# Edge stage: tile numbers and turns worked out in registers from two numbers a chunk, and the softmax links placed at later steps

## The reference, cut to what matters

```python
feat_src, feat_dst, feat_v = (feat @ W + b).reshape(N, HEADS, OUT_FEATS)   # three weights
e = el[src] + er[dst];  e = where(e >= 0, e, 0.2 * e)
e_max = segment_max(e, dst)
exp_e = exp(e - e_max[dst])
a = exp_e / maximum(segment_sum(exp_e, dst)[dst], 1e-16)
rst = segment_sum(feat_v[src] * a[:, :, None], dst)
x = x + rst + mix(xn);  x = x + ffn(layernorm(x))
```

## Time and profile before

| what | us |
|---|---|
| median of three runs | 3512.27 (3508.56 to 3518.39) |
| the profiled execution, its own time | 3480.26 |
| its span | 3478.4 |
| projection begins on TensorE | 99.85 |
| edge stage, first `turned_hot` to the last (L1124, 52 times) | 815.8 to 2376.1 |
| granted TensorE clock, mean over the span | 0.809 |

### The profile page before, as it was taken

One profiled execution on the slowest core, in us unless ns is written; L12 is line 12 of the kernel. 1 busy time (PEld: TensorE's weight loads), 2 busy tenths in 40 slices (PEclk: granted clock), 3 DMA queues, 4 the chain that ended last, 5 costly groups with the idle time before them and its releaser, 6 DMA issues. The chain is left out here.

```text
span 3478.4 us, 50828 instructions
## 1 busy us (share of the span) xinstructions
PE 2417.5 (69%) x11245; PEld 1803.3 (52%) x11246; DVE 1829.6 (53%) x3903; ACT 909.8 (26%) x1917; POOL 1338.1 (38%) x1406
## 2 busy tenths in 40 slices
PE   3899998666777877777877777777233329999500
PEld 3677776223555555555555555555233328888400
DVE  5544443786666655566556655565353334444433
ACT  0111111011333333333333333333443313333100
POOL 0000000302565555565556555652144342222244
PEclk8899998898888878888788878889555559999755
DMA  3122222644555555655656556653655634444576
GB/s 115 49 68 68 68 68 77 228 167 134 165 162 159 157 164 163 169 160 154 169 164 171 166 154 173 170 163 89 221 134 136 131 76 134 145 145 145 168 257 232
DMA packets 238264, 507.89 MB, mean 146 GB/s; under 512 B 50320, under 2 KB 76432, under 8 KB 238208
## 3 DMA queue, kind: packets, MB, share of 16 engines
q0 software_dynamic: 85936, 274.85, 28.6%
q1 hardware_dynamic: 134752, 196.94, 18.5%
q10 hardware_dynamic: 17520, 35.44, 3.0%
HBM read 394.73 MB, written 112.37 MB: 146 GB/s over the span
## 5 line engine op out<-in xcount | busy, mean ns | idle before, releaser
L618 POOL DMA_INDIRECT arena<-v_table,idx x832 | 917.2, 1102 | 847.1 <-PE ps L1566 670.1
L1566 PE MATMUL ps<-arena 128*128 128x260 f32 x3328 | 975.4, 441 | 315.9 <-issue 289.6
L1566 PEld LDWEIGHTS ps<-arena 128*128 128x128 f32 x3328 | 678.5, 216 | 533.2 <-issue 427.7
L757 ACT ACTIVATE arena<-ps x832 | 501.9, 603 | 1096.2 <-PE ps L1566 668.4
L1182 DVE TENSOR_TENSOR arena<-arena 128x512 f32<-128x512 f32 x832 | 547.1, 683 | 0.0
L1384 PE MATMUL ps<-arena 128*128 (+4 forms) x1994 | 423.8, 336 | 94.3 <-DMA arena<-q_table 73.8
L1389 PE MATMUL ps<-ident,arena 128*128 128x128 f32 x1128 | 213.8, 308 | 328.1 <-DVE arena L1257 257.2
L1384 PEld LDWEIGHTS ps<-arena 128*128 128x128 f32 (+1 forms) x1994 | 275.7, 195 | 224.8 <-issue 115.3
L1389 PEld LDWEIGHTS ps<-ident,arena 128*128 128x128 f32 x1128 | 151.0, 159 | 349.3 <-DVE arena L1257 262.2
L658 POOL DMA_INDIRECT arena<-xn_table,e_idx x105 | 99.3, 945 | 281.5 <-PE ps L1389 265.0
L595 POOL TENSOR_SCALAR ag<-ag 128x1 f32<-128x1 f32 x49 | 10.7, 219 | 502.3 <-DVE ag L999 502.2
(11 more groups left out here) (282 smaller groups left out, 3470.0 us busy)
## 6 DMA issues: line engine op xcount, KB each, us to landing
y_table<-arena SPq DMA_DIRECT2D x105, 256.0 KB, 2.5
arena<-local_table ACTq DMA_DIRECT2D x52, 512.0 KB, 4.2
arena<-in_x SPq DMA_DIRECT2D x98, 256.0 KB, 2.7
arena<-v_table,idx POOLq DMA_INDIRECT x832
v_table<-arena SPq DMA_DIRECT2D x49, 260.0 KB, 2.9
agg<-arena SPq DMA_DIRECT2D x49, 260.0 KB
arena<-agg SPq DMA_DIRECT2D x49, 260.0 KB, 4.6
x_mix<-arena SPq DMA_DIRECT2D x49, 256.0 KB, 2.7
```

Of the source, the lines that this page charges most:

```text
L618: pool.indirect_dma_start(vg[:, j % 2 * U + i, :], None, v_table, bass.IndirectOffsetOnAxis(ap=idx[:, j, i:i + 1], axis=0))\
L757: act.activation(halves(fin[:, bass.ds(dst_, DH)], HALF), halves(ps[:, bass.ds(src_, 2 * D)], D)[:, :, 0:HALF], ACT.Copy).then_inc(s("act_ ...
L1566: last = pe.matmul(ps[:, bass.ds(acc + h * D, HALF)], hot[:, i // V % 2, i % V, :], vg[:, b * U + i, h * HALF:(h + 1) * HALF], start=False ...
```

## The change: two numbers a chunk, and other places for the links

- The per-step tables go. Two tables with one entry a chunk take their place: `first_tab`, the node tile of the chunk's first step, and `turn_tab`, 16 bits that say which steps are turns. A loop turn of two chunks reads both (`chunk_places`): four entries of each on TensorE, two of each on VectorE and ScalarE.
- From them each engine works out the turn (`turn_of`: shift and mask), the next tile (`next_tile`: add), the accumulator (`room_of`: mask and product), and ScalarE the places and counts of `snapshot`. `tile_tab`, the step that ends each tile, stays and moves by one entry; a turn on TensorE reads it.
- A snapshot no longer waits for the matmul of its own step; it waits for the count of closed accumulators that its tile asks for.
- VectorE's links move: `scored` from behind step 2 to 5, `run_max` 4 to 7, `linked` 6 to 9, `joined_max` 9 to 11, `shifted` 12 to 13. TensorE's: `turned_e` 1 to 5, `gathered_ends` 3 to 7, `spread_ends` 5 to 9, `turned_max` 8 to 12, `factors` 10 to 11. ScalarE's: `factor` from behind snapshot 4 to 10, `weights` 10 to 12.
- VectorE makes the first `hot` tile of a chunk ahead of its wait for the exponentials, not behind it.
- The store count `fin_st` shares another semaphore.

```diff
-def chunks(eng, body, bases=None):
+def chunks(eng, body, places, ahead):
 
     for c in range(2):
-        body(c, c, 0, *(bases(c, 2) if bases else ()))
+        body(c, c, 0, places(c, ahead + 1))
     with eng.Fori(1, NCH // 2 - 1) as i:
-        own = bases(i * 2, 3) if bases else ()
+        own = places(i * 2, ahead + 2)
         for j in range(2):
-            body(i * 2 + j, j, i, *own[j:j + 2])
+            body(i * 2 + j, j, i, own[j:j + ahead + 1])
     for c in range(NCH - 2, NCH):
-        body(c, c % 2, c // 2, *(bases(c, 2) if bases else ()))
+        body(c, c % 2, c // 2, places(c, ahead + 1))
+
+
+def turn_of(eng, bits, i):
+
+    return eng.snap((bits >> i) & 1, min_val=0, max_val=1)
+
+
+def room_of(eng, d):
+
+    return eng.snap((d & 1) * (2 * D), min_val=0, max_val=2 * D)
+
+
+def next_tile(eng, d, turn):
+
+    return eng.snap((d + turn).with_bounds(min_val=0, max_val=NT - 1))
...
+        def chunk_places(engine, c, n):
+
+            return list(zip(looked_up(engine, first_tab, c, n, NT - 1), looked_up(engine, turn_tab, c, n, 2 ** U - 1)))
...
-            def snapshots(t, n):
-                places = looked_up(ENGINE.Activation, act_tab, t * 2, 2 * n, DUMMY * D)
-                counts = looked_up(ENGINE.Activation, act_tab, t * 2 + 2 * ST, 2 * n, 32768)
-                for i in range(n):
-                    (src_, dst_), (closed, stored) = places[2 * i:2 * i + 2], counts[2 * i:2 * i + 2]
-                    act.wait_ge(s("step_mm"), t + (i + 1))
-                    if later(t, 1) or i:
-                        act.wait_ge(s("act_step"), t + i)
-                    act.wait_ge(s("tile_sum"), closed)
-                    act.wait_ge(s("fin_st"), stored)
-                    act.activation(halves(fin[:, bass.ds(dst_, DH)], HALF), halves(ps[:, bass.ds(src_, 2 * D)], D)[:, :, 0:HALF],
-                                   ACT.Copy).then_inc(s("act_step"), 1)
-
-            def chunk(c, b, r):
+            def snapshot(t, d, turn):
+                src_ = act.snap(DUMMY * D - (DUMMY * D - (d & 1) * (2 * D)) * turn, min_val=0, max_val=DUMMY * D)
+                dst_ = act.snap(4 * DH - (4 * DH - (d & 3) * DH) * turn, min_val=0, max_val=4 * DH)
+                closed = act.snap(d + turn + 1, min_val=1, max_val=NT + 1)
+                stored = act.snap(d * 16 + past("fin_st", -16 * 3)[1], min_val=16, max_val=32768)
+                if later(t, 1):
+                    act.wait_ge(s("act_step"), t)
+                act.wait_ge(s("tile_sum"), closed)
+                act.wait_ge(s("fin_st"), stored)
+                act.activation(halves(fin[:, bass.ds(dst_, DH)], HALF), halves(ps[:, bass.ds(src_, 2 * D)], D)[:, :, 0:HALF],
+                               ACT.Copy).then_inc(s("act_step"), 1)
+
+            def chunk(c, b, r, own):
                 more = not (isinstance(c, int) and c == NCH - 1)
+                (d, bits), = own
                 if not (isinstance(c, int) and c >= NCH - 2):
                     chunk_in(c + 2, b)
-                snapshots(c * U, 4)
-                snapshots(c * U + 4, 1)
-                if more:
-                    factor(c + 1)
-                snapshots(c * U + 5, 4)
-                snapshots(c * U + 9, 2)
-                if more:
-                    weights(c + 1, 1 - b)
-                snapshots(c * U + 11, 4)
-                snapshots(c * U + 15, 1)
+                for i in range(U):
+                    last = not more and i == U - 1
+                    turn = 1 if last else turn_of(act, bits, i)
+                    snapshot(c * U + i, d, turn)
+                    if not last:
+                        d = next_tile(act, d, turn)
+                    if not more:
+                        continue
+                    if i == 10:
+                        factor(c + 1)
+                    elif i == 12:
+                        weights(c + 1, 1 - b)
...
+            d_r, turn, aux, bits = (row_[0:1, :] for row_ in row)
+            power_row, bits = bits[:, 0:U], bits[:, U:U + NCH]
+            for i in range(U):
+                dve.memset(power_row[:, i:i + 1], float(2 ** i))
+            dve.memset(turn[:, ST - 1:ST], 0.0)
             step_of(dve.tensor_scalar(d_r, d128[0:1, :], 1.0 / P, None, ALU.mult))
...
             step_of(dve.tensor_tensor(turn[:, 0:ST - 1], d_r[:, 1:], d_r[:, 0:ST - 1], ALU.subtract))
...
+            in_chunks = [row_.rearrange("o (c i) -> o c i", i=U) for row_ in (turn, aux)]
+            step_of(dve.tensor_tensor(in_chunks[1], in_chunks[0], power_row.unsqueeze(1).broadcast_to([1, NCH, U]), ALU.mult))
+            step_of(dve.tensor_reduce(bits, in_chunks[1], AX.X, ALU.add))
+            dve.tensor_copy(turn_tab[0:1, 0:NCH], bits)
+            dve.memset(turn_tab[0:1, NCH:NCH + 2], 0)
+            dve.tensor_copy(first_tab[0:1, 0:NCH], d_r[:, 0:ST:U])
+            dve.memset(first_tab[0:1, NCH:NCH + 2], 0)
             dve.wait_ge(s("start_mm"), 1)
...
+            dve.memset(tile_tab[0:1, 0:1], 1)
+            dve.tensor_copy(tile_tab[0:1, 1:NT], bank[7][0:1, 0:R_])
+            dve.memset(tile_tab[0:1, NT:NT + 1], ST).then_inc(s("tabs_ready2"), 1)
...
+            def found(t, i):
+                wait_past(dve, s("step_mm"), t, V + 1)
+                dve.tensor_tensor(hot[:, i // V % 2], col_no[:].unsqueeze(1).broadcast_to([P, V, P]),
+                                  dst_local[:, bass.ds(t, V)].unsqueeze(2).broadcast_to([P, V, P]), ALU.is_equal)
+
+            def step(i, b):
                 v = halves(vg[:, b * U + i, :], HALF)
                 weighed(v, v, v[:, :, D // 2:]).then_inc(s("step_pv"), 1)
 
-            def chunk(c, b, r, base, _):
+            def chunk(c, b, r, own):
                 more = not (isinstance(c, int) and c == NCH - 1)
                 n, q = 1 - b, (r if b == 0 else r + 1)
-                dve.wait_ge(s("p_exp"), c + 1)
                 for i in range(U):
-                    step(c * U + i, i, b)
+                    if i % V == 0:
+                        found(c * U + i, i)
+                    if i == 0:
+                        dve.wait_ge(s("p_exp"), c + 1)
+                    step(i, b)
                     if i == 1 and later(c, 1):
-                        rescaled(c, base)
+                        rescaled(c, room_of(dve, own[0][0]))
                     if not more:
                         continue
-                    if i == 2:
+                    if i == 5:
                         scored(c + 1, n, q)
-                    elif i == 4:
+                    elif i == 7:
                         run_max(c + 1, n)
-                    elif i == 6:
+                    elif i == 9:
                         linked(c + 1)
-                    elif i == 9:
+                    elif i == 11:
                         joined_max(c + 1, n)
-                    elif i == 12:
+                    elif i == 13:
                         shifted(c + 1, n)
                     elif i == 14:
                         factored(c + 1)
...
-            def tiles_of(c):
-                return looked_up(ENGINE.PE, d_tab, c * U, U, NT - 1)
-
-            def expanded(c, tiles):
+            def expanded(c, d, bits):
                 pe.wait_ge(s("hot_t"), c + 1)
                 wait_past(pe, s("e_sub"), c, 1)
-                for i, d in enumerate(tiles):
+                for i in range(U):
                     last = product(prep[:, i * 3 * H:(i + 1) * 3 * H],
-                                   [(hot_t[:, i * P:(i + 1) * P], er_flat[:, bass.ds(d * 3 * H, 3 * H)])])
+                                   [(hot_t[:, i * P:(i + 1) * P], er_flat[:, bass.ds(d * (3 * H), 3 * H)])])
+                    if i < U - 1:
+                        d = next_tile(pe, d, turn_of(pe, bits, i))
...
-            marks = []
-
-            def step(t, i, b):
-                if i % V == 0:
-                    marks[:] = looked_up(ENGINE.PE, pe_tab, t * 2, 2 * V + 1, 2 * D)
-                acc, turn, other = marks[i % V * 2:i % V * 2 + 3]
+            def step(t, i, b, d, turn):
+                acc = room_of(pe, d)
                 pe.wait_ge(s("step_pv"), t + 1)
                 for h in range(2):
                     last = pe.matmul(ps[:, bass.ds(acc + h * D, HALF)], hot[:, i // V % 2, i % V, :],
                                      vg[:, b * U + i, h * HALF:(h + 1) * HALF], start=False, stop=False)
                 last.then_inc(s("step_mm"), 1)
+                other = ((acc + 2 * D) & (4 * D - 1)).with_bounds(min_val=0, max_val=2 * D)
                 with pe.If(turn):
                     empty(acc, False, True).then_inc(s("tile_sum"), 1)
-                    freed, = looked_up(ENGINE.PE, pe_tab, t + (2 * ST + 2), 1, ST)
+                    freed, = looked_up(ENGINE.PE, tile_tab, d, 1, ST)
                     pe.wait_ge(s("act_step"), freed)
                     empty(other, True, False)
...
-                    if i == U - 1 and ahead:
-                        tiles = tiles_of(c + 2)
```

(26 more changed lines are left out.)

62 lines of the change are left out of this document (12 added, 50 removed).

## The result

The changed kernel took 4152.71 us (median of 4 runs, 4136.57 to 4162.47; the profiled execution 4144.77, its span 4142.9); beside it on the same chip the kernel before took 3514.82 us. The ratio is 1.181 (95% interval 1.1765 to 1.186): 18% slower, where 3351 us and a range of 3200 to 3460 us were forecast. The same program, run again on two other chips, took 3765 us (ratios 1.081 and 1.083), and 4144 us in a later run on a chip where the kernel before took 3513 us (1.178). So two things are to be explained: 283 us that come on every chip that it ran on (3764.9 - 3481.6), and 388 us more that come on some chips only, of which the kernel before shows 33.

A forecast was written before the change was run, and what follows sets the result against it. A ring of waits between VectorE and TensorE, with no engine full, was taken to set the edge stage's pace. 50 x 2.9 = 145, + 13 + 3 = 161 us saved gave 3351 us (median), range 3200 to 3460 us.

The forecast's parts named there:

- ScalarE under the period: Edge stage, ScalarE: register arithmetic of 0.45 us a step runs beside the activation, at worst 19 us a chunk.
- the forecast's whole period: Edge stage: one chunk takes 27.8 us, with the clock low in about four chunks of five; 2.9 us less.
- The last term: Edge stage, VectorE from `run_max` to the end of `joined_max`, with latency: 7.5 us of the period.
- `joined_max` to L1578: Edge stage, from the end of `joined_max` on VectorE to the rescaled accumulator on TensorE: 10.6 us.
- my upper bound: TensorE's `expanded`: two more register instructions per product, 0.31 us each, 5.0 us a chunk; 0.23 and 3.6 us expected.
- rival 2: Edge stage: arithmetic costs more in `expanded` and the steps, 29.8 us a chunk, 3451 us; chance 0.15.
- L1578 to `run_max`: Edge stage, TensorE from rescaled accumulator to transposed scores: 6.7 us at full clock, 10.5 us with it low.
- the transposed scores: Edge stage, VectorE: its wait for TensorE's transpose of the scores grows to 4 to 8 us a chunk.
- The wait for the transposed maximum: Edge stage, VectorE before `shifted`: a new wait for TensorE's transpose of about 0.9 us a chunk.
- Chunk 0 loses two loads of 16: Start of the edge stage: two loads of 16 go, mostly hidden behind the first gathers; 3 us saved.
- Rival 3: Edge stage: clock stays low, the transpose wait replaces the accumulator's; period 32.0 us, 49 us more, 3561 us; chance 0.07.
- the 161 us: Whole kernel, total saving: 145 us in the edge stage, 13 us of table building, 3 us in chunk 0.

The follow-up runs named there:

- experiment 3: Changed kernel with ScalarE's two snapshot addresses worked out ahead of its waits, not behind them; 3493.2 us, ratio 1.003.
- experiment 9: Changed kernel with one number changed: ScalarE's `factor` stands behind snapshot 6 instead of 10; 3521.9 us, ratio 1.012.
- experiment 5: The changed kernel itself, unedited, run again on another chip; 3764.9 us, ratio 1.081.
- the first trace: Profiled execution of the changed kernel's first run, unedited; 4144.77 us, median of that run 4152.71 us, ratio 1.181.
- 8: Changed kernel with links back at the kernel before's steps and ScalarE on tables, TensorE and VectorE on registers; 3399.3 us, ratio 0.976.
- 7: Changed kernel with links back at the kernel before's steps and ScalarE's snapshot addresses worked out ahead of its waits; 3385.3 us, ratio 0.972.
- experiment 12: Changed kernel with shorter address arithmetic on ScalarE, placed ahead of the waits, and links half way between early and late places; 3347.9 us, ratio 0.962.

## Why the prediction was wrong

**The step that failed: ScalarE under the period.** "On ScalarE some 20 operations are four or five fused instructions, 0.45 us a step; the activation of 0.60 us runs beside them. At worst they follow it: 16 x 1.2 = 19 us, still under the period." They are 17 instructions, 1.18 us for the 16 that follow the activation: 16 x 1.78 = 28.5 us, more than the 27.8 us of the forecast's whole period. Shown by experiment 3, where order alone brings a snapshot to 1.29 us and the kernel 272 us down, from 3764.9 to 3493.2.

**The step left out: `factor` and `weights` in the ring.** The last term, "`linked` 1.2, steps 10 and 11 1.2, `joined_max` 2.0 ...: 7.5 us", runs past `factor` on ScalarE as if it cost nothing, though the change puts it behind snapshot 10. Measured from the start of `run_max` to the end of `joined_max`, this term is 13.3 us in experiment 5 and 20.0 us in the first trace. (These terms are means over the 49 chunks, from the starts and ends of the operations named.) To hold ScalarE's whole 28.5 us against the period would have missed this even with the right number: what counts is what stands between its two link operations. Shown by experiment 9.

**Mis-sized: `joined_max` to L1578 (L1581 before).** Forecast 10.6 us, measured 14.4 us (13.6 in experiment 3). Two parts of it show in TensorE's order of time (experiment 5): the steps before the boundary run at the low clock after the wait for `hot_first`, and the products of `expanded` start 0.34 us apart, not 0.23, so that all 16 take 4.4 to 4.8 us instead of 3.6. (The granted clock was 0.50 from 1700.0 to 1705.5 us and 0.55 from 1703.4 to 1710.3.)

```profile
1700.40 0.59 PE L1383 MATMUL ps<-diag,hot_first 8*128 8x8 f32 x2 [5.74 <-DVE hot_first L1149]
1703.47 2.09 PE L1560 MATMUL ps<-arena 128*128 128x260 f32 x4 [2.48 <-DVE arena L1177]
...
1705.57 4.79 PE L1560 MATMUL ps<-arena 128*128 128x260 f32 x12
1710.30 0.83 PE L1549 MATMUL ps<-zeros 1*128 1x260 bf16 x6
...
1711.55 0.18 PE L1383 MATMUL ps<-arena 128*128 x1 [0.15 <-issue]
1711.89 0.18 PE L1383 MATMUL ps<-arena 128*128 x1 [0.15 <-issue]
```

12 matmuls in 4.79 us stand against 2.89 us in the earlier trace rows. A product has two plain register instructions of 36 ns and a fused one of 63 ns. That is the two more that were my upper bound, and the 0.34 us lie above its 0.31: rival 2's mechanism was there, with a chance of 0.15.

**Right.** L1578 to `run_max` is 9.1 us (27.8 - 10.6 - 7.5 = 9.7 forecast), the transposed scores cost 363.2/49 = 7.4 us (4 to 8 forecast), rows 0.5 us and the accumulator 0.7 us a chunk (both near nothing). The mean clock is 0.79 in experiment 5. The wait for the transposed maximum is 2.1 us, where I had 0.9. "Chunk 0 loses two loads of 16 ..., 3 us" did not come: between the first two `turned_hot` the changed kernel is 3.0 us slower.

**The rivals.** Rival 3, the slower one, was not what happened: its condition was more than 12.9 us from the accumulator to the transposed scores, and that is 9.1. The sign was missed because every rival looked at VectorE and TensorE; rival 3 had the sign right for another reason, with a chance of 0.07. Without ScalarE in the way (experiment 3) the change as a whole comes to 1.003, so that even then the 161 us were not there. With early places the rest of the change gave 82 to 96 us (8 and 7), and the late places took 108 us back (3 against 7). The 388 us that came on some chips only are outside the forecast's sum: the trace of the kernel before, from which it was worked out, has no slow register instruction.

## What to carry to other kernels

When an operation is moved, write down for every engine that it crosses what stands between the two ends of its chain there, idle engines too; a ring through an engine that is busy 22% of the time held this kernel. Before counting register arithmetic as hidden, ask on which side of the engine's own waits it is emitted: work out addresses ahead of the waits, fold constants into the form with the fewest instructions, and count the instructions in a trace, not in the source. A table in memory costs 0.21 to 0.25 us a value; the 16 register instructions between two activations cost as much as five values (1.18 us).

## What the runs showed of the hardware

- **A long loop body of ScalarE is fetched anew in every turn, a longer one of TensorE is not.** ScalarE's bodies of 214 and 222 instructions go with 32 packets of the instruction queue in the whole program, those of 336 with 150 and those of 592 with 202 or more. With the long ones ScalarE's sequencer stands some 3 us after the loop's branch, where it stands 0.2 us in the kernel before; first the kernel before, then experiment 5, and third TensorE's branch in experiment 5:

```profile
L122 ACTq COMPARE_BRANCH  x1: 50/50/50, 1692.1 to 1692.1; - x1
L122 ACTq FUSED_REGOPS  x1: 83/83/83, 1692.3 to 1692.3; - x1
```

```profile
L122 ACTq COMPARE_BRANCH  x1: 54/54/54, 1601.5 to 1601.5; - x1
L122 ACTq FUSED_REGOPS  x1: 73/73/73, 1604.5 to 1604.5; - x1
```

```profile
L122 PEldq COMPARE_BRANCH  x1: 208/208/208, 1604.8 to 1604.8; - x1
L122 PEldq FUSED_REGOPS  x1: 63/63/63, 1605.1 to 1605.1; - x1
```

  TensorE goes on 0.06 us after its branch, in the kernel before too. Its turn has over 580 recorded instructions there and over 750 in experiment 8, and both have 32 packets.

  The Trainium skill has this in Runtime: NRT & Kernel Launch, section Instruction fetch mechanics: a taken branch whose target lies outside the window of two pages of 256 instructions forces a fetch before execution goes on, and TensorE's instruction memory is four times that of most engines. The traces agree for both engines; that ScalarE's body of 336 is fetched too shows that its window doesn't reach back 512 instructions. It cost little where ScalarE was off the path: experiment 7, with 203 packets, is not slower than 8, with 32 (3385 and 3399 us, of which 8 has some 11 us of table building more). In experiment 5 it lies on the ring: from `weights` to the next `factor` it takes 32.6 us with the loop's branch and loads and 28.0 us without.
- **The same program ran 10% apart on chips where the kernel before differed by 0.9%.** 3765 us twice and 4144 to 4153 us twice, each with its own ratio against the kernel before on the same chip. A single chip's ratio is no full answer for a kernel whose path lies on a sequencer.
- Whether the best kernel (experiment 12, 0.962) keeps its gain on a chip with the slow register instructions was not seen.
